# Two gated attention layers on one core: the last batch's key stacks in other memory, and its row maxima sent in two halves

## What is computed

```
x = x + tanh(g_xattn[0]) * cross_attention_8_heads_of_64(layernorm(x), ctx)          # stream X
x = x + tanh(g_ffn[0])   * (self_attention_16_heads_of_8(h) + moe_8_experts_top2(h)) # stream F, h = layernorm(x)
x = x + tanh(g_xattn[1]) * cross_attention_16_heads_of_8(layernorm(x), ctx)          # keys: K, the rest: B
x = x + tanh(g_ffn[1])   * moe_8_experts_top2(layernorm(x))                          # stream C
```

## Time and profile before

| | us |
|---|---|
| median of 3 runs | 752.22 (744.86 to 756.33) |
| the profiled execution, its own time | 746.59 |
| its span, first to last instruction | 744.8 |
| outside the span | 1.8 |
| PE busy | 663.1 (89%) |
| DVE busy | 569.7 (76%) |
| ACT busy | 374.2 (50%) |
| POOL busy | 344.5 (46%) |
| mean granted TensorE clock | 0.933 |

### The profile page before, as it was taken

How to read it: one execution, slowest core, us unless ns; L and a number is a source line. 1 busy time by engine, 2 the same in 40 slices (tenths; PEclk the granted TensorE clock), 3 DMA queues, 4 the chain that set the end, 5 groups by cost and what they waited for, 6 DMA issues and landing times.

```text
span 744.8 us, 13302 instructions
## 1 busy us (share of the span) xinstructions
PE 663.1 (89%) x5232; PEld 336.2 (45%) x5232; DVE 569.7 (76%) x1055; ACT 374.2 (50%) x482; POOL 344.5 (46%) x467
## 2 busy tenths in 40 slices
PE   6699898998999899989999999989999789787684
PEld 2265454553544455434645355534653424333342
DVE  2626578589998879788898979887888987928534
ACT  4064345545546753775357644765357346263360
POOL 4273753852463257415663368326764324422233
PEclk9599999999999999989999999999999969969597
DMA  7210202112101221121121311121013221021000
GB/s 193 80 58 19 86 1 62 45 44 63 43 24 41 77 64 52 52 79 32 41 66 42 99 48 65 36 75 50 22 58 97 71 68 68 4 89 55 7 1 14
DMA packets 45790, 40.82 MB, mean 55 GB/s; under 512 B 4824, under 2 KB 37536, under 8 KB 45728
## 3 DMA queue, kind: packets, MB, share of 16 engines
q1 hardware_dynamic: 45168, 39.52, 17.1%
q10 hardware_dynamic: 560, 0.46, 0.2%
HBM read 22.93 MB, written 17.04 MB: 54 GB/s over the span
## 4 chain that ended last, share of the span: by engine, by line
PE 66%; DVE 21%; ACT 6%; issue 2%; POOL 2%; DMA 2%; SPq 1%; POOLq 0%; DVEq 0%
PE psum L670 13%; PE psum L626 7%; PE psum L590 7%; DVE mx8B L925 7%; PE psum L582 6%; DVE mxA L831 4%; PE psum L658 4%; ACT probB L740 4%; PE psum L557 3%; PE psum L639 3%; PE psum L551 3%; PE psum L600 2%; PE psum L577 2%; DVE rden L839 2%; PE psum L675 2%
## 5 line engine op out<-in xcount | busy, mean ns | idle before, releaser
L925 DVE TENSOR_REDUCE mx8B<-psum 128x2 f32<-128x1024 f32 x128 | 153.7, 1219 | 22.7 <-PE psum L639 21.5
L740 ACT ACTIVATE probB<-psum 128x1024 f32<-128x1024 f32 x128 | 126.4, 1029 | 57.2 <-PE psum L658 56.5
L727 ACT ACTIVATE probX<-psum 128x1024 f32<-128x1024 f32 x64 | 65.5, 1024 | 95.1 <-PE psum L582 94.8
L920 DVE TENSOR_REDUCE mx8F<-psum 128x4 f32<-128x1024 f32 x64 | 77.0, 1217 | 8.8 <-PE psum L633 8.6
L831 DVE TENSOR_REDUCE mxA<-psum 128x2 f32<-128x1024 f32 x64 | 76.6, 1216 | 8.5 <-PE psum L564 8.1
L839 DVE RECIPROCAL rden<-psum 128x256 f32<-128x256 f32 x32 | 56.1, 1752 | 34.8 <-PE psum L594 34.7
L740 ACT ACTIVATE probF<-psum 128x1024 f32<-128x1024 f32 x64 | 65.1, 1026 | 24.0 <-PE psum L658 22.2
L999 POOL TENSOR_TENSOR prodC<-prodC 128x256 f32<-128x256 f32 x30 | 21.8, 725 | 104.6 <-DVE prodC L913 102.3
L670 PE MATMUL psum<-probB,v8B 128*32 128x256 f32 x1024 | 67.5, 408 | 2.8 <-ACT probB L740 2.7
L582 PE MATMUL psum<-qX,kX 64*128 64x256 f32 x512 | 68.4, 388 | 0.0
L991 POOL TENSOR_TENSOR psum_k<-probX 128x512 f32<-128x512 f32 x32 | 40.8, 1274 | 59.5 <-ACT probX L727 58.5
(11 more groups left out here) (192 smaller groups left out, 1174.2 us busy)
## 6 DMA issues: line engine op xcount, KB each, us to landing
k8B<-k_dK SPq DMA_DIRECT2D x32, 192.0 KB
k_dK<-partsK SPq DMA_DIRECT2D x8, 384.0 KB, 2.5
q8F<-q_dF SPq DMA_DIRECT2D x32, 96.0 KB
k8F<-k_dF SPq DMA_DIRECT2D x32, 96.0 KB
q8B<-q_dB SPq DMA_DIRECT2D x32, 96.0 KB
k_dK<-partsK SPq DMA_DIRECT2D x8, 256.0 KB, 2.7
cTX<-in_ctxT SPq DMA_DIRECT2D x8, 192.0 KB, 2.8
cTK<-in_ctxT SPq DMA_DIRECT2D x8, 192.0 KB, 2.4
```

The lines of the kernel that those rows point to most:

```text
L727: nc.scalar.activation(prob[s][(8 * b + k) % SLOTS[s]][:], ps, ACT.Exp, scale=float(XD) ** -0.5).then_inc(done["ACT"], 1)
L740: nc.scalar.activation(prob[s][(units * b + k) % SLOTS[s]][:], ps, ACT.Exp, scale=float(D8) ** -0.5).then_inc(done["ACT"], 1)
L920: nc.vector.tensor_reduce(mx8[s][:].rearrange("p t (i q) -> p i t q", i=2)[:, :, :, k], ps.rearrange("p (i t n) -> p i t n", i=2, t=QT), A ...
L925: nc.vector.tensor_reduce(mx8[s][:, t, :].rearrange("p (i q) -> p i q", i=2)[:, :, p], ps.rearrange("p (i n) -> p i n", i=2), AX.X, ALU.ma ...
```

## The change

All of it is for batch 7; the other batches keep their steps.

1. The keys and values of B are projected from X's copy of the context (`cTX`), which nothing overwrites after batch 7 of X. The second read (`cTK`) of batch 7 and its waits go.
2. B's query stack of batch 7 lies in F's `q8`. Its key stack lies in F's `k8` (first half: pairs 0 to 3, viewed as 4 x 512 instead of 8 x 256) and in `kXb`, X's bf16 keys (second half). These are free when F's last `e8` and X's last `mx` matmuls are done, so the wait for B's `e8` of batch 6 goes, in the plan and in the code. POOL fills `kXb` with ones (job `ones`, semaphore `padded`) after X's last `mx`.
3. In F and B of batch 7 the maxima are transposed, written and read back in two halves (`PARTS`): `mT8`, `mw` and `mr` come twice, each half after half of the `mx8` pieces, with a second tile `m2b` and semaphores of its own. `e8` of the first four head pairs waits for the first half only.
4. For that, the order of heads in `mx8` is changed from (i q) to (g i q) in all batches, and the read `mr` of the other batches takes two chunks of a row instead of one.

```
+LAST = BATCH - 1
+PARTS = (1,) * (BATCH - 1) + (2,)
...
+    if s == "K" and b == LAST:
+        p.job("POOL", s, "ones", b, 0, 2.2, ("PE", "X", "mx", b, 7))
     for k in range(2):
-        p.job("SP", s, "sr", b, k, 2.6 if s == "F" else 1.3, ("SP", s, "sw", b, 0), ("PE", *old, b - 1, (4 if s == "F" else 8) * k + 3 + 4 * (s != "F")))
+        free = ("PE", *old, b - 1, (4 if s == "F" else 8) * k + 3 + 4 * (s != "F"))
+        if s != "F" and b == LAST:
+            free = ("POOL", "K", "ones", b, 0) if s == "K" and k else ("PE", "F", "e8", b, NPAIR - 1)
+        p.job("SP", s, "sr", b, k, 2.6 if s == "F" else 1.3, ("SP", s, "sw", b, 0), free)
...
-    p.fill("DVE", 0, s, "mT8", b, 0, .26, .85, [("DVE", s, "mx8", b, maxima - 1)], [("SP", s, "mw", b - 1, 0)])
-    p.job("SP", s, "mw", b, 0, .35, ("DVE", s, "mT8", b, 0), ("SP", s, "mr", b - 1, 0))
-    p.job("SP", s, "mr", b, 0, 1.25, ("SP", s, "mw", b, 0), ("PE", s, "e8", b - 1, units - 1))
+    parts = PARTS[b]
+    for k in range(parts):
+        p.fill("DVE", 0, s, "mT8", b, k, .26, .85, [("DVE", s, "mx8", b, maxima // parts * (k + 1) - 1)], [("SP", s, "mw", b - 1, 0)])
+        p.job("SP", s, "mw", b, k, .35, ("DVE", s, "mT8", b, k), ("SP", s, "mr", b - 1, 0))
+        p.job("SP", s, "mr", b, k, 1.25, ("SP", s, "mw", b, k), *[("PE", s, "e8", b - 1, units - 1)] * ((s, b) != ("B", LAST)))
...
-        p.fill("ACT", 1, s, "e8", b, k, .32, 1.03, [("SP", s, "mr", b, 0)], [("PE", s, "pv8", g // units, g % units // n)])
+        p.fill("ACT", 1, s, "e8", b, k, .32, 1.03, [("SP", s, "mr", b, parts * k // units)], [("PE", s, "pv8", g // units, g % units // n)])
...
+        def queries(s, b):
+
+            return q8["F" if (s, b) == ("B", LAST) else s]
+
+        def keys(s, b, rows, p):
+
+            if (s, b) != ("B", LAST):
+                return k8[s][rows, p, :]
+            if p < NPAIR // 2:
+                return k8["F"][rows, 2 * p:2 * p + 2, :].rearrange("r o n -> r (o n)")
+            return kXb[rows, p - NPAIR // 2, :]
...
-                sp.wait_ge(*is_full(to, "e8", b - 1, NPAIR * KEYS[to] // SEQ // 2 * (k + 1) - 1))
+                if (to, b) != ("B", LAST):
+                    sp.wait_ge(*is_full(to, "e8", b - 1, NPAIR * KEYS[to] // SEQ // 2 * (k + 1) - 1))
+                else:
+                    sp.wait_ge(*is_full("F", "e8", LAST, NPAIR - 1))
+                    if s == "K" and k:
+                        sp.wait_ge(padded, 1)
...
-                    pe.wait_ge(*after("K", "ctx", b))
-                    last = mm(ps[:, 0:KV], wk8["B"][:], cT["K"][:, :], start=True, stop=True)
+                    pe.wait_ge(*after(context(b), "ctx", b))
+                    last = mm(ps[:, 0:KV], wk8["B"][:], cT[context(b)][:, :], start=True, stop=True)
...
+                    if PARTS[b] == 2 and p >= NPAIR // 2:
+                        pe.wait_ge(S[s]["mr1"], 32)
...
+                if name == "ones":
+                    pool.wait_ge(*is_full("X", "mx", b, 7))
+                    engine.memset(kXb[:], 1.0).then_inc(padded, 1)
```

More of the change, by code:

```diff
@@ L149, in plan_f, with context @@
                 [("DVE", "F", "wb", b, 0), ("POOL", "B", "xb", b - 1, 0), ("DVE", "B", "xh", b - 1, 0)])
+def context(b):
+    return "K" if b < LAST else "X"
 def plan_k(p, b):
-    p.job("SP", "K", "ctx", b, 0, .4, ("PE", "K", "kk", b - 1, 0), ("PE", "K", "vv", b - 1, 1))
-    p.fill("ACT", 0, "K", "kk", b, 0, 1.0, 1.4, [("SP", "K", "ctx", b, 0)], [("SP", "K", "sw", b - 1, 0)])
+    if b < LAST:
+        p.job("SP", "K", "ctx", b, 0, .4, ("PE", "K", "kk", b - 1, 0), ("PE", "K", "vv", b - 1, 1))
+    p.fill("ACT", 0, "K", "kk", b, 0, 1.0, 1.4, [("SP", context(b), "ctx", b, 0)], [("SP", "K", "sw", b - 1, 0)])
     plan_stack(p, "K", b, 3.9, 3, ("ACT", "K", "kk", b, 0), ("B", "e8"))
     for k in range(2):
-        p.fill("DVE", 0, "K", "vv", b, k, .58, .43, [("SP", "K", "ctx", b, 0)], [("PE", "B", "pv8", b - 1, 3)])
+        p.fill("DVE", 0, "K", "vv", b, k, .58, .43, [("SP", context(b), "ctx", b, 0)], [("PE", "B", "pv8", b - 1, 3)])
 def plan_b(p, b):
@@ L482, in load_parts @@
                     if s != "K":
-                        engine.dma_start(q8[s][rows, pairs, :].rearrange("r p n -> r (p n)"),
+                        engine.dma_start(queries(s, b)[rows, pairs, :].rearrange("r p n -> r (p n)"),
                                          q_d[s].rearrange("j (i d p) n -> i d j p n", i=2, p=NPAIR)[i, :, :, pairs]
@@ L486, in load_parts @@
                     if s != "B":
-                        engine.dma_start(k8[to][rows, pairs, :].rearrange("r p n -> r (p n)"),
+                        stack = k8[to][rows, pairs, :]
+                        if (to, b) == ("B", LAST):
+                            stack = kXb[rows, :, :] if k else k8["F"][rows, :, :]
+                        engine.dma_start(stack.rearrange("r p n -> r (p n)"),
                                          k_d[s].rearrange("j (i d p) n -> i d j p n", i=2, p=NPAIR)[i, :, :, pairs]
@@ L613, in _ @@
                     else:
-                        pe.wait_ge(*after("K", "ctx", b))
+                        pe.wait_ge(*after(context(b), "ctx", b))
                     for j in range(2):
                         c = 2 * k + j
-                        tok = xT["F"][:, c * P:(c + 1) * P] if s == "F" else cT["K"][:, c * P:(c + 1) * P]
+                        tok = xT["F"][:, c * P:(c + 1) * P] if s == "F" else cT[context(b)][:, c * P:(c + 1) * P]
                         last = mm(ps[:, j * P:(j + 1) * P], tok, wv8["F" if s == "F" else "B"][:], start=True, stop=True)
@@ L638, in _ @@
                         for i in range(2):
-                            last = mm(ps[:, KV * i:KV * (i + 1)], q8[s][64 * i:64 * i + KROWS, p, t * P:(t + 1) * P],
-                                      k8[s][64 * i:64 * i + KROWS, p, :], start=True, stop=True)
+                            last = mm(ps[:, KV * i:KV * (i + 1)], queries(s, b)[64 * i:64 * i + KROWS, p, t * P:(t + 1) * P],
+                                      keys(s, b, slice(64 * i, 64 * i + KROWS), p), start=True, stop=True)
                 elif name == "mT8":
-                    pe.wait_ge(*is_done(s, "mx8", b, NPAIR * KEYS[s] // SEQ - 1))
+                    n = H8 // PARTS[b]
+                    pe.wait_ge(*is_done(s, "mx8", b, NPAIR * KEYS[s] // SEQ // PARTS[b] * (k + 1) - 1))
                     for t in range(QT):
-                        last = transpose(ps[0:H8, t * P:(t + 1) * P], mx8[s][:, t, :], ident[:])
+                        last = transpose(ps[0:n, t * P:(t + 1) * P], mx8[s][:, t, n * k:n * (k + 1)], ident[:])
                 elif name == "wT":
@@ L658, in _ @@
                             last = mm(ps[:, 512 * i + SEQ * c:512 * i + SEQ * (c + 1)],
-                                      k8[s][64 * i:64 * i + MROWS, p, (c0 + c) * P:(c0 + c + 1) * P],
-                                      q8[s][64 * i:64 * i + MROWS, p, :], start=True, stop=True)
+                                      keys(s, b, slice(64 * i, 64 * i + MROWS), p)[:, (c0 + c) * P:(c0 + c + 1) * P],
+                                      queries(s, b)[64 * i:64 * i + MROWS, p, :], start=True, stop=True)
                 elif name == "pv8":
@@ L918, in _ @@
                     dve.wait_ge(*is_full(s, "mT8", b - 1))
[L919 to L926 removed]
+                    p, t = (k, slice(0, QT)) if s == "F" else (k // QT, slice(k % QT, k % QT + 1))
+                    nc.vector.tensor_reduce(
+                        mx8[s][:].rearrange("p t (g i q) -> p g i t q", g=2, i=2)[:, p // 4, :, t, p % 4],
+                        ps.rearrange("p (i t n) -> p i t n", i=2, t=QT if s == "F" else 1), AX.X, ALU.max, negate=True).then_inc(drained, 1)
                 elif name == "mT8":
                     dve.wait_ge(*after(s, "mw", b - 1))
[L929 to L930 removed]
+                    rows = H8 // PARTS[b]
+                    to = (m2b if k else m2)[s]
+                    link(s, nc.vector.tensor_copy(to[0:rows, 0, :], ps[0:rows, 0:SEQ]))
+                    nc.vector.tensor_tensor(to[0:rows, 1, :], ps[0:rows, 0:SEQ], to[0:rows, 0, :], ALU.subtract).then_inc(drained, 1)
         @block.gpsimd
```

46 lines of the change are left out of this document (25 added, 21 removed).

## The result

| | before | after |
|---|---|---|
| median of 20 runs, us | 752.72 | 747.21 |
| lowest and highest, us | 744.86, 757.82 | 742.27, 755.16 |
| profiled execution, us | 746.59 | 752.49 |
| its span, us, and mean granted clock | 744.8, 0.933 | 750.7, 0.929 |

The ratio is 0.9931, 95% interval [0.9902, 0.996]: 5 us faster where 17.5 were forecast, inside the 2% that counts as no change. The two profiled executions stand the other way round. That of before is among its fastest runs, that of after among its slower ones, so no difference of their spans is a gain. A further profile of before, taken later (`before_again`: 751.77 us, span 749.9, clock 0.919), is the better partner for a profile at 752.49, and I use both.

A forecast was written before the change was run, and what follows sets the result against it. PE bounds the long middle; at the end exps and maxima take turns. Overlap 12, F's lead 5 and keys 1, less 0.5 for second trips, gave 17.5 us: from the median 734.7, written as 734, range 722 to 748.

The forecast's parts named there:

- the 9.9 us by which the maxima were to start sooner: Part 2, B of batch 7: with other stack memory the first maxima matmul runs at 664.6 instead of 674.47.
- F's lead: F of batch 7: with halves, four of eight units run from 609, so F ends sooner; bounds 0 and 13, taken 5 us.
- rival (d): All batches: the planner deals the lists anew and waits at batch turns grow; slower, up to 766 us; chance 0.06.
- ACT has finished batch 6 by 677: End of the kernel: batch 6's exps are over before batch 7's first `e8`, forecast at 683.4 instead of 700.67.
- The overlap, 12 us: B of batch 7: earlier maxima in two halves beside exps end the last `pv8` at 711.5, a gain of 12 us.
- the keys, 1 us: Part 1, start of batch 6's exps: without the second context read, up to 1.7 us gained, counted as 1; drains hidden.
- done at 693.5: B of batch 7: the second half's maxima end at 693.5 and its first `e8` runs at 699.5.
- Rival (a): B of batch 7: the maxima stretch to 31 us from 664.6; gain 10, band 5 to 13, time 742; chance 0.30.
- By then ACT has had 16 us for the eight exps of the first half, so they are gone: B of batch 7: at 0.95 us each, the first half's exps finish before the second half's first `e8` at 699.5.
- Its floor was ACT's 34.8 us: From 658 to 724: ACT's work keeps the last `pv8` from ending before 694.7; gain at most 29, or 27 with gaps.
- rival (c): SP's queue or PE's order: a new wait replaces the old one; 0 to 4 us left, 750; chance 0.09.
- the first case: The forecast's own case, the whole kernel: gain 14 to 22 us, 17.5 as the sum; chance 0.47.

The follow-up runs named there:

- h3_change_late_keys: The change with the old head order and read in batches 0 to 6, batch 7's keys not before batch 6's ninth maxima piece: 0.9962 of before.
- e7_old_ranks_old_heads: The change with the old head order and read in batches 0 to 6, jobs ranked by the ways of before: 1.0008 of before, 751.28 us.
- f2_end_and_f_halves: `f1_end_only` with the halves in F of batch 7 added: 0.9928 of before, 746.45 us.
- f1_end_only: Before plus parts 1 and 2 and halves in B only, old read and ways, keys not before batch 6's ninth maxima piece: 0.9983, 748.47 us.
- f3_early_keys: `f1_end_only` without the bound on batch 7's keys, so the planner places them freely: 1.0045 of before, 755.06 us.
- e6_change_old_heads: The change in its own lists, with the old head order and read of the maxima in batches 0 to 6: 0.9913 of before, 745.26 us.
- e5_heads_only: Before with part 4 alone in all batches, every engine's list as before: 1.0066 of before, 756.53 us.

## Why the prediction was wrong

In short: the sum laid its steps on the timeline of before, which the planner did not keep. Of its terms, the 9.9 us by which the maxima were to start sooner measured 6.8; the tail behind the last maximum took 22.2 us for 18.0, as the sum had no term for PE's work; and F's lead of 5 us did not show.

**The planner's lists.** The first step that failed is the sentence against rival (d): "nearly every way of batches 0 to 6 ends through the same chain of B, and loses the same amount, so the order of ways stays". The ways fell unevenly and the lists changed from batch 2 on. It did not cost 31.5 us as that rival priced it, but it broke the frame of the sum, which laid the steps on the timeline of before. "ACT has finished batch 6 by 677" is such a row: with batch 6's maxima 12.5 us behind F's output and not 2.1, its exps began at 679.44 and ended at 701.8. Lists by the ways of before gave 1.00 and the re-dealt ones 0.993 with the same steps, so the re-dealing is not the loss either; it is why the steps don't meet the rows they were costed from.

**The overlap, 12 us, and the keys, 1 us: 5.3 to 6.6.** That the maxima would run beside the exps, that ACT's 21 us hole would go, and that two round trips would be made, all came. Of the three stretches in the table above, two were mis-sized.

The start: 18.7 us behind F's output and not 15.6. Against 664.6 the first maxima matmul came at 677.94, 13.3 us late and 3.5 later than before, as the queries that it needs were written only at 669.18. 10.3 us of this is F's own output; from there to the write 9.9 us passed, where they were 8.3, and from the write to the matmul 8.8, where 7.3 were forecast. Of the eight profiles with parts 2 and 3 in B, seven have the start 18.6 to 18.9 us behind F's output (`h3_change_late_keys` 19.9), so this term is 6.8 us against before, and not 9.9.

The maxima: 28.4 us and not 28.9, so "done at 693.5" failed by its start alone. In part this was luck. The sum had 10.7 us of other DVE work between them; there were 5.6 us, and 4.0 us in which DVE was idle, mostly for PE, whose order puts `e8` and `pv8` of batch 6 between the maxima matmuls. Rival (a) had 31 us for this, which was not far off either.

The tail: 22.2 us from the last maximum to the end of the last `pv8`, and not 18.0. "By then ACT has had 16 us for the eight exps of the first half, so they are gone" failed. The first half was done at 690.47, and its first `e8` ran at 704.50, 14.0 us later and not 6.0, as PE's order has batch 6's `e8` and `pv8` and expert products of C first; the ninth unit's `e8`, at 712.85, met ACT still at the first half's. What the sum left out is PE. Its floor was ACT's 34.8 us, but from the first maxima matmul to the end of the last `pv8` PE was busy, by the profile, 46.35 of 50.59 us, where it had been busy 38.00 of 49.10, and the forecast for that stretch was 46.9 in all. From F's output to the last `pv8`, seven of the same eight profiles take 67.7 to 69.3 us, whatever their lists (`h3_change_late_keys` 73.6).

**F's lead, 5 us: none to be seen.** "Four of the eight units could run from 609 on" failed. F's first maxima of batch 7 were transposed at 622.09, where in before all of them were at 611.62, so its first `e8` of batch 7 ran at 631.79 and not at the 622.53 of the earlier trace rows; the second half was transposed at 632.12 and read back at 636.33. No profile with F's halves has F's output before the 652.8 of `before_again`: they have it at 653.2 to 664.2. In `e7_old_ranks_old_heads` both writes are early and the second read stands behind the stack reads of B (SP):

```profile
621.50 0.29 SPq L566 DMA_DIRECT2D m_dF<-m2bF  x1
622.49 0.54 SPq L581 DMA_DIRECT2D q8F<-m_dF  x2
626.03 1.38 SPq L538 DMA_DIRECT2D k8B<-k_dK  x2
627.46 1.33 SPq L531 DMA_DIRECT2D q8B<-q_dB  x2
628.83 0.74 SPq L581 DMA_DIRECT2D q8F<-m_dF  x2
```

This is the place in SP's order that rival (c) named, but in F and not in B, and nothing waited for it: PE came to the fifth `e8` unit of F only at 647.08, by its list. So what kept F from a lead there is PE's order, in which the eight units stand 25.6 us apart (629.39 to 654.97), where they stood 17.2 apart in before (622.53 to 639.75). The queries of batch 7 follow F's output, so what F lost came out of the earlier buffer: they were written at 669.18 and not at 657.28. The runs leave room for a small lead: `f2` against `f1`, 0.5%, with overlapping intervals.

**Part 4: unpriced.** The prediction costs parts 1 to 3 and leaves the new order of heads out. Alone it is 0.66%, under a third of the forecast gain. Within the change it is 0.2% by the two ratios and not to be told from nothing.

**The keys "hidden".** The projection's drains were hidden, but its place was not free: 0.6% in `f3_early_keys` against `f1_end_only`, 0.8% in `e7_old_ranks_old_heads` against `f2_end_and_f_halves`, nothing in the re-dealt lists.

**The profile's standing.** "It lies 5.6 us below the median" was taken as an offset that both kernels share. It was one execution with a good clock. Over the 20 runs of after the time follows the mean granted clock: 742.27 to 743.9 us at 0.946 to 0.947, 752.94 to 755.16 at 0.921 to 0.930. Equal clocks give after no lead: of the runs at 0.930 to 0.937, the 5 of after take 749.3 us in the mean, and 14 of before, on the experiments' four chips, 747.3. The gain of the medians is that after has a higher clock more often, 0.937 in the mean of its runs, where before's median run on each of the four chips has 0.920 to 0.922. Whether the shorter waits of PE at the end bring this about is not shown. The prediction counted the clock inside its 12 us, and its sign, above 0.8 from 651 on, did not come: 658 to 675 was at 0.51. The Trainium skill (TensorE: Matmul & The Clock Gate, Part 1) has activity release the clock; the row of 658 to 675 agrees, 0.51 with PE busy 7.97 of 17 us.

**The number.** 747.21 us lies inside the range of 722 to 748, near its upper end, and the gain of 5 us in the band of rival (a). That is not (a) borne out: (a) started its 31 us at 664.6 and had F's lead in it, and neither came. Two misses of the first case's own, the start and the tail, and F's missing lead brought the time there.

**What held.** The maxima's length was as summed, and the second trip from the last maximum to the ninth `e8` took 6.5 us (706.38 to 712.85) for 6.0. The memset on POOL and SP's new wait cost nothing to be seen: the stack reads they guard are issued from 651.01 to 653.8, the queries not before 671.86. The second round trips issue in 0.54 us. The rest behind the last `pv8` went from 21.2 to 22.2 us.

**Open.** How much of what was lost ahead of F's output is the change's and how much one execution's; why part 4 costs 5 us alone and not in the change; why some kernels lose the clock at 124 to 132 us; whether F's halves are worth their 0.5%; which of `e6_change_old_heads`, `f2_end_and_f_halves` and after is the fastest, as their intervals overlap.

## What to carry to other kernels

Where a planner deals the order of the work, run the planner's own code over both plans and compare the lists before costing anything: a change of one batch's steps changed half the places of PE's list here. Its value was nothing in the lists of before, 0.7% with one job placed later in them, and 2% or more against the re-dealt lists without it. An idle hole of one engine between two phases isn't there to be taken whole: the phase moved beside another stretches (20 us to 28), by other work on its own engine and by waiting for the one that feeds both, so add up the busy time of every engine over the new overlap. Here PE's 46 us were the tighter bound, not ACT's 34.8. Price every part of a diff, a layout change that touches all batches above all, and take more than one profile of before where single runs spread over 13 us.

## What the hardware showed unexpectedly

A DMA of the same bytes took SP 0.63 us to issue with two chunks for each row of its access pattern (`e5_heads_only`), and 0.25 us with one (`before_again`; 16 each, spread under 0.06 us but for one of 0.40).

The same kernel on the same inputs (after, 20 runs) ran at mean granted clocks from 0.921 to 0.947, and its time went from 755.16 to 742.27 us with it. Of the two profiles of before, what the mean clock lacks of the full one is (1 - 0.933) x 744.8 = 49.9 us and (1 - 0.919) x 749.9 = 60.7 us. The lower level is half the clock, so the time spent at it is twice that, 100 and 121 us. The spans differ by 5.1 us for 21.6: about a quarter of a microsecond of span for each one at the lower level, by an estimate from two executions.
